# One LN, attention and FFN layer on eight cores: transposes evicted by one engine, and the closing stage moved into the FFN's down projection

## The reference

```
xn  = layernorm(X)                                   # no weights
x2  = layernorm(xn) * ln_w + ln_b
q, k, v = split(x2 @ W_in);  q, k = rope(q), rope(k) # 16 heads of 128
att = softmax(q k^T / sqrt(128)) v @ W_out + xn
h   = silu(xn @ Wg^T) * (xn @ Wu^T)                  # 8192 wide
ffn = h @ Wd^T       # Wg, Wu, Wd = (integer - 128) * scale per row
out = X + att + ffn                                  # so: X + xn + (...)
```

## Time and profile before

| what | us |
|---|---|
| median of 3 runs (3055.06 to 3055.35) | 3055.31 |
| profiled execution | 3057.66 |
| its span on the slowest core (core 1) | 3056.1 |
| spans of the 8 cores | 3039.6 to 3056.1 |
| granted PE clock of the cores, mean share of full speed | 0.939 to 0.945 |
| PE busy | 2592.9 |
| ACT busy | 851.2 |
| DVE busy | 613.1 |
| POOL busy | 385.3 |

### The profile page before, as it was taken

The page is one execution under the profiler, slowest core; times in us unless marked ns, Lnnn a source line. Parts: engine busy times, 40 slices in busy tenths (PEclk is TensorE's granted clock), DMA queues, the critical chain, the costliest instruction groups (busy, mean ns, idle before and its releaser), DMA issues.

```text
span 3056.1 us, 37325 instructions; the slowest of 8 cores (3039.6 to 3056.1 us)
## 1 busy us (share of the span) xinstructions
PE 2592.9 (85%) x12552; PEld 1241.5 (41%) x12552; DVE 613.1 (20%) x931; ACT 851.2 (28%) x1402; POOL 385.3 (13%) x388
## 2 busy tenths in 40 slices
PE   4446898898989898986989999989999999989940
PEld 2222544444453535442434444434444444434410
DVE  4652242424333342422000000000000000000023
ACT  5770436262625344361111111100011111100001
POOL 2231101101010101000011111100011111101000
PEclk9667999999999999997989999999999999999975
DMA  4112202111020202005043343333433343434424
GB/s 126 56 62 83 83 22 62 46 39 56 29 63 22 83 1 77 1 1 190 31 158 146 139 164 138 138 138 141 163 138 138 149 154 138 157 119 151 152 96 151
DMA packets 57578, 305.61 MB, mean 100 GB/s; under 512 B 6964, under 2 KB 7092, under 8 KB 31672
## 3 DMA queue, kind: packets, MB, share of 16 engines
q1 hardware_dynamic: 57400, 303.23, 27.5%
HBM read 294.81 MB, written 8.39 MB: 99 GB/s over the span
## 4 chain that ended last, share of the span: by engine, by line
PE 84%; DMA 5%; DVE 4%; issue 3%; ACT 3%; POOL 1%; SPq 0%; DVEq 0%; ACTq 0%; POOLq 0%
PE pu L919 15%; PE pg L901 14%; PE pg L974 7%; PE pu L974 7%; PE pp L483 6%; PE ppC L483 6%; PE ppC L615 4%; PE po L796 4%; PE pp L615 4%; PE ppC L671 3%; PE pst L344 3%; PE ppD L679 3%; PE pp L653 2%; DMA fxt<-xb 2%; PE ppR L503 1%
## 5 line engine op out<-in xcount | busy, mean ns | idle before, releaser
L901 PE MATMUL pg<-xnfm,wstage 128*128 128x512 bf16 x2048 | 464.6, 380 | 6.8 <-DMA wstage<-gbp 6.8
L919 PE MATMUL pu<-xnfm,wstage 128*128 128x512 bf16 x2048 | 464.3, 380 | 3.0 <-DMA wstage<-ubp 3.0
L901 PEld LDWEIGHTS pg<-xnfm,wstage 128*128 128x128 bf16 x2048 | 200.7, 98 | 251.0 <-issue 10.8
L919 PEld LDWEIGHTS pu<-xnfm,wstage 128*128 128x128 bf16 x2048 | 200.6, 98 | 245.9 <-issue 5.3
L931 POOL TENSOR_TENSOR hfm<-sgp,sup 128x512 bf16<-128x512 f32 x128 | 162.0, 1265 | 1092.1 <-ACT sup L927 1092.1
L910 ACT ACTIVATE sgp<-pg,gsc_sb 128x512 f32<-128x512 f32 x128 | 88.2, 689 | 591.3 <-PE pg L901 591.3
L664 ACT ACTIVATE ebig<-pp,biasc 128x512 bf16<-128x512 f32 x352 | 233.6, 688 | 40.7 <-PE pp L653 36.5
L974 PE MATMUL pg<-wstage,hfm 128*128 128x512 bf16 x1024 | 231.5, 384 | 13.8 <-DMA wstage<-dwp 13.8
L452 POOL CAST wbf<-wf 128x512 bf16<-128x512 f32 x192 | 119.0, 624 | 873.3 <-PE ppC L483 516.1
L974 PE MATMUL pu<-wstage,hfm 128*128 128x512 bf16 x1024 | 227.7, 379 | 0.0
L483 PE MATMUL pp<-xn2f,wbf 128*128 128x512 bf16 x768 | 174.3, 382 | 32.4 <-POOL wbf L452 32.1
(11 more groups left out here) (108 smaller groups left out, 2263.7 us busy)
## 6 DMA issues: line engine op xcount, KB each, us to landing
wstage<-gbp SPq DMA_DIRECT2D x64, 1024.0 KB, 5.4
wstage<-ubp SPq DMA_DIRECT2D x64, 1024.0 KB, 7.4
wstage<-dwp SPq DMA_DIRECT2D x32, 2048.0 KB, 7.8
wf<-wip SPq DMA_DIRECT2D x192, 256.0 KB, 2.9
xt<-xb SPq DMA_DIRECT2D x16, 1024.0 KB, 10.2
wof<-wop SPq DMA_DIRECT2D x8, 2048.0 KB, 9.7
fxt<-xb SPq DMA_DIRECT2D x8, 1024.0 KB, 6.8
out<-fin SPq DMA_DIRECT2D x8, 1024.0 KB, 4.7
```

What stands on the lines that cost most here:

```text
L901: m = prog.op(T, lambda e, h=hc, i2=ic2, p=par, t=tg, s=psl: e.matmul(pg[s][:, :], gb2[p][:, h * 256 + i2 * 128: h * 256 + i2 * 128 + 128] ...
L919: m = prog.op(T, lambda e, h=hc, i2=ic2, p=par, t=tg, s=psl: e.matmul(pu[s][:, :], ub2[p][:, h * 256 + i2 * 128: h * 256 + i2 * 128 + 128] ...
```

## The change

There are two edits. In `_emit_ln` all evictions of transposes go to DVE; the instructions on ACT are gone. And the closing stage is no longer called. In its place the down projection, behind POOL's sum of each block of 128 rows and 512 columns, loads the block of X into xst (256 KB, one buffer), has ACT compute X * (rstd + 1) + nmr = X + xn into one PSUM bank (sst, named "pfs"), has DVE add this to acc, and stores the block of acc. r1p holds rstd + 1. The function `_emit_final` stays in the file but isn't called.

```diff
--- before.py
+++ after.py
@@ -219,10 +219,8 @@
             _emit_outproj(env)
             prog.barrier()
         if stage >= 4:
-            _emit_ffn(env)
+            _emit_ffn(env, xb if stage >= 5 else None)
             prog.barrier()
-        if stage >= 5:
-            _emit_final(env, xb)
 
         prog.barrier()
         st_total = prog.dcnt.get("st", 0)
@@ -346,35 +344,19 @@
                                waits=wts)
                 last_t = mm_t
                 if kind == "x2":
-                    if dc % 2 == 0:
-                        ev = prog.op(V, lambda e, t=tt, d=dc, pp=p: e.tensor_scalar(
-                                         xn2[:, d * S + t * 128: d * S + (t + 1) * 128],
-                                         pp[:, 0:128], lnw[:, d:d + 1], lnb[:, d:d + 1],
-                                         ALU.mult, ALU.add),
-                                     waits=[(T, mm_t)])
-                        slot_ev[pslot] = (V, ev)
-                    else:
-                        ev = prog.op(Sc, lambda e, t=tt, d=dc, pp=p: e.activation(
-                                         xn2[:, d * S + t * 128: d * S + (t + 1) * 128],
-                                         pp[:, 0:128], AF.Identity,
-                                         bias=lnb[:, d:d + 1], scale=lnw[:, d:d + 1]),
-                                     waits=[(T, mm_t)])
-                        slot_ev[pslot] = (Sc, ev)
+                    ev = prog.op(V, lambda e, t=tt, d=dc, pp=p: e.tensor_scalar(
+                                     xn2[:, d * S + t * 128: d * S + (t + 1) * 128],
+                                     pp[:, 0:128], lnw[:, d:d + 1], lnb[:, d:d + 1],
+                                     ALU.mult, ALU.add),
+                                 waits=[(T, mm_t)])
                     x2ev_pair[dc % 2] = ev
                 else:
-                    if dc % 2 == 0:
-                        ev = prog.op(Sc, lambda e, t=tt, d=dc, pp=p: e.activation(
-                                         xnfm[:, d * 1024 + t * 128: d * 1024 + (t + 1) * 128],
-                                         pp[:, 0:128], AF.Copy),
-                                     waits=[(T, mm_t)])
-                        slot_ev[pslot] = (Sc, ev)
-                    else:
-                        ev = prog.op(V, lambda e, t=tt, d=dc, pp=p: e.tensor_copy(
-                                         xnfm[:, d * 1024 + t * 128: d * 1024 + (t + 1) * 128],
-                                         pp[:, 0:128]),
-                                     waits=[(T, mm_t)])
-                        slot_ev[pslot] = (V, ev)
-            env["x2ev"][tt] = [(V, x2ev_pair[0]), (Sc, x2ev_pair[1])]
+                    ev = prog.op(V, lambda e, t=tt, d=dc, pp=p: e.tensor_copy(
+                                     xnfm[:, d * 1024 + t * 128: d * 1024 + (t + 1) * 128],
+                                     pp[:, 0:128]),
+                                 waits=[(T, mm_t)])
+                slot_ev[pslot] = (V, ev)
+            env["x2ev"][tt] = [(V, x2ev_pair[1])]
             src_free[sl] = last_t
 
...
-def _emit_ffn(env):
+def _emit_ffn(env, fxb=None):
     nc, prog, dram = env["nc"], env["prog"], env["dram"]
     xnfm, acc = env["xnfm"], env["acc"]
+    do_final = fxb is not None
+    rstd, nmr = env["rstd"], env["nmr"]
...
+        if do_final:
+            xst = Ls("xst0", [128, 512], F32)
+            sst = ctx.enter_context(nc.psum_tensor("pfs", [128, 512], F32))
+            r1p = Ls("r1p", [128, 16], F32)
...
+        ax_prev = 0
+        ad_prev = 0
+        if do_final:
+            r1p_seq = prog.op(V, lambda e: e.tensor_scalar(r1p[:, :], rstd[:, :],
+                                                           1.0, None, ALU.add))
+            outp = dram["out"]
...
                     tmp_free = ga
                     acc_g = ga
                     pd_free[tb] = [(V, tv)]
+                    if do_final:
+                        tbg = tg * 4 + tb
+                        ld = prog.dma("sync", lambda e, tt=tbg, f=fg: e.dma_start(
+                                          out=xst[:, :],
+                                          in_=fxb[tt * 128:(tt + 1) * 128,
+                                                  f * 512:(f + 1) * 512]),
+                                      sem="ldp0", waits=[(Sc, ax_prev)])
+                        ax = prog.op(Sc, lambda e, tt=tbg: e.activation(
+                                         sst[:, :], xst[:, :], AF.Identity,
+                                         bias=nmr[:, tt:tt + 1],
+                                         scale=r1p[:, tt:tt + 1]),
+                                     waits=[("ldp0", ld), (V, ad_prev),
+                                            (V, r1p_seq)])
+                        ad = prog.op(V, lambda e, tt=tbg, f=fg: e.tensor_add(
+                                         acc[:, tt * D + f * 512: tt * D + f * 512 + 512],
+                                         acc[:, tt * D + f * 512: tt * D + f * 512 + 512],
+                                         sst[:, :]),
+                                     waits=[(Sc, ax), (G, ga)])
+                        prog.dma("sync", lambda e, tt=tbg, f=fg: e.dma_start(
+                                     out=outp[tt * 128:(tt + 1) * 128,
+                                              f * 512:(f + 1) * 512],
+                                     in_=acc[:, tt * D + f * 512:
+                                             tt * D + f * 512 + 512]),
+                                 sem="stp", waits=[(V, ad)])
+                        ax_prev = ax
+                        ad_prev = ad
             sg_free = tmp_free
...
-        if debug:
+        if do_final:
+            prog.op("sync", lambda e: e.nop(), waits=[("stp", prog.dcnt["stp"])])
+        if debug and not do_final:
```

## The result

| | median us | runs | ratio to before (95%) |
|---|---|---|---|
| before | 3056.8 | 10 | |
| after | 3113.3 | 10 | 1.0185 (1.0168 to 1.0201) |

Slower by 1.85%, some 56 us. The forecast was 3132 us in 3092 to 3180; the time lies in the range, 19 us under the number. Two of the ten runs of the changed kernel had a lower clock on one or both dies (3302.5 and 3431.3 us); the other eight took 3106.8 to 3125.4 us, with a median of 3110.4, and the ratios, like all medians further down, leave such runs out. The profiled execution took 3107.5 us with a span of 3105.9, on core 6; before's span was 3056.1.

The account below looks back on a forecast made before the run. Layer norm engines were taken to alternate, TensorE to bound the middle and to have no work in the last stage. 66 + 110 + 10 - 110 = +76 us on a median of 3055.3 gave 3132 us, range 3092 to 3180.

Parts of the forecast that it names:

- part one: Layer norm: DVE evicting all transposes lengthens the four batches' phases, +66 us, all on the path.
- six seams: Between down projection groups: weights issued late behind serial blocks; TensorE 16.5 us late plus 1.9 slow, six times, +110 us.
- seam between halves: Between the token halves: gate and up weight loads are issued later, behind the last blocks, +10 us.
- end: After TensorE's last matmul: the separate last stage goes, span ends at 2946.4 instead of 3056.1, -110 us.
- Rival C: Block chain: loads beside stores take 4.4 us instead of 2.9, +36 us, 3168 us, with other slowdowns about 3197; 12%.
- The sign named for this: Down projection blocks: a step is wrong if xst lands outside 2.5 to 3.6 us.
- I take 0.48 and 0.33: Layer norm: assumed us from start to start of DVE's evictions (L350) and casts (L372).
- the lower bound, 43 us: Layer norm: cost of DVE taking all evictions at the bare durations, 0.41 and 0.29 us.
- a sign of a wrong step: Layer norm: a step is wrong if the evictions' pitch is under 0.41 or over 0.55 us.
- Rival B: Layer norm: DVE keeps pace with the transposes, phases stay as long, this part is free, 3066 us; 5%.
- The estimate from the Trainium skill: Layer norm: 120 cycles plus one per element at 0.96 GHz, 258 ns a tile; DVE would keep up, 3066 us.
- Rival A: Down projection: seams are hidden because next weights get out while a store waits, 3011 us, faster; 4%.

Follow-up runs that it names:

- e1: Kernel before with only the changed layer norm (all transpose evictions on DVE), the closing stage left as before: 3072.4 us, ratio 1.0044.
- e9: Changed kernel with its single xst buffer, the next block's load issued ahead of this block's store: 3063.7 us, ratio 1.0024 to before.
- e5: Changed kernel with two xst buffers and two PSUM banks, each load ahead of the store two blocks before: 3059.8 us, ratio 1.0007 to before.
- e6: Kernel before with the closing stage folded in, two xst buffers; SP issues two block loads, next weights, then stores: 2967.8 us, ratio 0.9705.
- e11: As e6, but all four block loads precede the next weights, and gate and up loads precede stores between halves: 2947.2 us, ratio 0.9642 to before.
- e10: Kernel before, evictions still shared by DVE and ACT, with 8 PSUM slots instead of 4 for the transposes: 3050.6 us, ratio 0.9977.
- e2: Changed kernel with the layer norm of before, so only the closing stage moves into the down projection: 3109.4 us, ratio 1.0157 to before.
- e4: Changed kernel with the next group's first two weight loads ahead of the four load and store pairs: 3074.6 us, ratio 1.0052 to before.
- e7: Kernel before with all transpose evictions on ACT: 3068.1 us, one run, no interval.
- e3: Kernel before with all transpose evictions on DVE and 8 PSUM slots instead of 4 for the transposes: 3063.5 us, ratio 1.0017.

## Why the prediction was right, and where a term was off

| term | forecast us | measured us | from |
|---|---|---|---|
| part one | +66 | +13 | e1 |
| six seams | +110 | 6 x (19.5 + 2.2) = +130 | after: waits; 32 matmuls in 8.63 to 9.76 for 7.08 |
| seam between halves | +10 | (16.95 + 1.86) - (3.00 + 1.36) = +14 | waits for gate and up weights and the slow 16 behind them |
| end | -110 | 11.4 - 119.5 = -108 | end of the last matmul to end of span |
| sum | +76 | +49 (span: +49.8) | |

**The seams.** The mechanism is shown: the order on SP makes them, since e9, e5, e6 and e11 remove them step by step by moving loads. (e5, e6 and e11 also have a second buffer; whether the order of e11 works with one buffer was not run.) The term was 3.3 us a seam short, and that lies in the chain of a block: behind a store xst landed in 3.65 us on average (3.08, 3.09 and 4.58 at the seam shown), against 2.9 taken from wf, and ACT's scaling took 0.78 for 0.69; stores came 6.0 us apart, not 4.94. Rival C (loads beside the store ahead of them land later) was right in kind, at half the size it gave. The sign named for this, landings outside 2.5 to 3.6 us, showed in 11 of the 24.

**Part one.** The failed step is "I take 0.48 and 0.33": the pitch of back-to-back evictions. A run of three L350 without a noted wait seemed to show DVE's own pace, but 0.485 us is the time of two transposes, of which DVE took one; it stays 0.47 with eight slots (e10). The page's own row had the hint, 17.4 us of DVE's idle time before L350 put down to PE. Even the lower bound, 43 us, failed, because it took an instruction's duration as the least distance between two starts. Batches grew by 4.4 us (batch 1) and 3.1 us (batch 2), not by 19.6 and 13.4, and DVE's own pitch of 0.32 us is under the 0.41 that the prediction named as a sign of a wrong step. Rival B, DVE keeping pace so that this part is free (5%), came nearer than the forecast did: the true cost is a fifth of 66 us. The estimate from the Trainium skill (VectorE: DVE Perf Modes, section on the TRN2 errata), 258 ns, lies between the pitches measured, 0.32 us with pointer operands and 0.20 us for a cast; the 410 ns that the prediction held against it are a duration, which says nothing of the pitch.

**The end** was right within 2 us. **Rival A**, seams that are hidden, did not occur in this order of instructions; e11 shows that it was available, with the same arithmetic and one order changed.

The errors had opposite signs (-53 in part one; +20, +4 and +2 in the seams and the end), which is why the total came close: the ledger ends 27 us under the forecast's +76, and the medians 19 or 20, since the profiled run is one of the fastest of the changed kernel. That was luck: the total was right with a split that was not.

The store ahead of a load accounts for part of its lateness: in e5 block 2's load, which has none just ahead, landed in 2.5 to 2.8 us on the profiled core, and block 3's, 0.5 us behind a store, in 3.0 to 4.4. What stays open is why these spread so (3.0 to 5.1 us in the changed kernel); what the other cores' transfers do to them was not separated. And e2 costs more than after's ledger gives for part two; its blocks' loads were slower (3.7 us behind a store, for 3.4), for which no run here gives a reason.

## What to carry to other kernels

A stage that is folded into a loop brings its DMAs into the loop's queue: ask for each one what it waits for and what stands behind it, and put every load that can go early ahead of every store that must wait. A hoisted load can itself be the one that waits (e4), so follow the queue once more after each move. An instruction's duration in a trace is not the distance between two starts: compare count times mean with the group's busy time before using it as a rate.

## What the runs showed of the hardware

DVE and ACT rows overlap when they stand back to back: 414 ns and 0.32 us from start to start on DVE, 555 ns and 0.35 us on ACT (e7), for 128x128 from PSUM with per-partition scale and bias; 319 ns and 0.20 us for the cast with eight slots (e3). DVE's 0.32 is the same with four slots and eight, and with TensorE at 1.2 and at 2.4 GHz. Float32 transposes of 128x128 start every 0.24 us with eight PSUM slots (64 in 15.40 us, e10), again at either level, though the row of one lasts 447 ns at the lower (changed kernel) and 300 at the higher; four slots make it 0.26 (16.81 us). A load of 256 KB that is issued less than 0.5 us behind one of 2 MB lands 8.0 to 9.6 us after its issue (changed kernel and e4), one behind a store of 256 KB in 3.0 to 5.1, and one with neither just ahead in 2.5 to 2.8 (e5).
